# The exponential of the clipped source flow, made on VectorE from the tanh of both flows

## The reference

```python
conserved_sink   = sum((q + EPS) * (k_so_sum + EPS), -1) + EPS
conserved_source = clip(sum((k + EPS) * (q_si_sum + EPS), -1) + EPS, -1.0, 1.0)
sink_allocation    = sigmoid(conserved_sink)
source_competition = softmax(conserved_source, -1) * n      # over the tokens
v_comp = v * source_competition[..., None]
kv  = einsum('bhnd,bhnm->bhdm', k, v_comp)
out = einsum('bhnd,bhdm->bhnm', q_norm, kv) * sink_allocation[..., None]
```

## Time and profile before

| | |
|---|---|
| median of 3 runs | 2896.59 us (2896.01 to 2897.06) |
| the profiled execution, its own time | 2897.44 us |
| its span, from the first instruction to the last | 2895.7 us |
| outside of the span | 1.7 us |
| mean granted clock of TensorE | 0.944 |
| instructions | 67341 |

### The profile page before, as it was taken

How to read it: one execution, slowest core, us unless ns; L and a number is a source line. 1 busy time by engine, 2 the same in 40 slices (tenths; PEclk the granted TensorE clock), 3 DMA queues, 4 the chain that set the end, 5 groups by cost and what they waited for, 6 DMA issues and landing times. The chain is left out here.

```text
span 2895.7 us, 67341 instructions
## 1 busy us (share of the span) xinstructions
PE 2512.6 (87%) x26720; PEld 1816.3 (63%) x26720; DVE 2187.3 (76%) x3781; ACT 1440.4 (50%) x2616; POOL 704.7 (24%) x593
## 2 busy tenths in 40 slices
PE   4898889988898888998889979898798997989979
PEld 2666557665576656765667656676566765666646
DVE  4857778678777787776977769768697585985868
ACT  2755237552466434664256632567336572265813
POOL 1220332204322042220512205112152021520125
PEclk8999999999999999999999989999899998999989
DMA  5110211102111021110211112010120101201012
GB/s 218 38 37 2 84 48 38 37 2 95 37 38 37 2 99 34 41 34 6 98 30 45 30 38 73 26 46 27 41 76 27 45 19 52 66 29 48 14 55 70
DMA packets 93371, 136.26 MB, mean 47 GB/s; under 512 B 10111, under 2 KB 55240, under 8 KB 92552
## 3 DMA queue, kind: packets, MB, share of 16 engines
q1 hardware_dynamic: 84872, 115.16, 12.2%
q0 software_dynamic: 8192, 16.79, 1.9%
HBM read 101.31 MB, written 30.61 MB: 46 GB/s over the span
## 5 line engine op out<-in xcount | busy, mean ns | idle before, releaser
L1025 DVE TENSOR_REDUCE neg_max<-ps 128x1 f32<-128x1024 f32 x512 | 622.8, 1216 | 51.0 <-PE ps L1454 39.7
L700 ACT ACTIVATE probs<-ps,neg_max 128x1024 f32<-128x1024 f32 x512 | 571.1, 1116 | 158.2 <-DVE neg_max L1025 156.7
L1454 PE MATMUL ps<-keys,q_parts 64*128 64x512 f32 x3072 | 523.5, 448 | 82.7 <-ACT probs L700 56.6
L1331 PE MATMUL ps<-q_parts,w_split 128*128 128x512 f32 x1536 | 458.7, 434 | 68.7 <-DVE ffn L1147 41.0
L1331 PEld LDWEIGHTS ps<-q_parts,w_split 128*128 128x128 f32 x1536 | 281.7, 190 | 220.1 <-DVE ffn L1143 119.1
L599 POOL TENSOR_TENSOR probs<-ffn,q_parts 128x512 f32<-128x512 f32 x208 | 291.5, 1404 | 490.8 <-DMA q_parts<-gate_rows 276.9
L1475 PEld LDWEIGHTS ps<-ident,probs 64*128 64x128 f32 x8192 | 348.1, 143 | 96.0 <-ACT probs L700 17.2
L1454 PEld LDWEIGHTS ps<-keys,q_parts 64*128 64x128 f32 x3072 | 265.4, 196 | 220.8 <-ACT probs L700 108.3
L754 ACT ACTIVATE ffn<-ffn 128x512 f32<-128x512 f32 x256 | 159.9, 630 | 462.2 <-DVE ffn L1143 461.5
L1033 DVE COPY probsT<-ps 128x512 f32<-128x512 f32 x512 | 348.1, 680 | 23.6 <-PE ps L1475 23.6
L1475 PE MATMUL ps<-ident,probs 64*128 64x64 f32 x8192 | 350.2, 227 | 16.2 <-ACT probsT L682 16.2
(11 more groups left out here) (213 smaller groups left out, 3320.0 us busy)
## 6 DMA issues: line engine op xcount, KB each, us to landing
w_split<-w_parts SPq DMA_DIRECT2D x132, 256.0 KB, 2.6
q_parts<-gate_rows SPq DMA_DIRECT2D x64, 512.0 KB, 4.4
y_rows<-probs SPq DMA_DIRECT2D x40, 256.0 KB, 2.2
x_in<-in_x SPq DMA_DIRECT2D x9, 512.0 KB, 4.1
w_parts<-q_parts SPq DMA_DIRECT2D x2, 2048.0 KB, 14.4
out<-x_mid SPq DMA_DIRECT2D x8, 512.0 KB, 3.2
ffn<-in_gate_up SPq DMA_DIRECT2D x1, 2048.0 KB, 8.9
probsT<-in_gate_up SPq DMA_DIRECT2D x1, 2048.0 KB, 13.2
```

Of the source, the lines that this page charges most:

```text
L700: nc.scalar.activation(probs[:, t % 3, :], banks(2 * (t % 2)), ACT.Exp, bias=neg_max[:, t % 4:t % 4 + 1], accum_out=row_sum[:, g % 2, t % ...
L1025: nc.vector.tensor_reduce(neg_max[:, t % 4:t % 4 + 1], banks(2 * (t % 2)), X, ALU.max, negate=True).then_inc(max_ready.sem, 1)
L1331: mm = nc.tensor.matmul(ps[:, bank, :], w_split[:, f % CHUNK_SLOTS, h, k * P:(k + 1) * P], tokens[:, half], start=(part == 0), stop=(part ...
L1454: mm = nc.tensor.matmul(ps[:, 2 * (t % 2) + c, :], q_parts[rows, j, q, n * P:(n + 1) * P], keys[rows, k, :], start=(part == 0), stop=(part ...
```

## The change

ScalarE takes the tanh of both flows at once, in place, in one instruction of 256 columns, and no exponential. For the source flow, VectorE then works out `exp(x) = (1 + t) / (1 - t)` with `t = tanh(x / 2)`: `1 - t`, its reciprocal, and the product with `1 + t`. The clip to -1 and 1 keeps t away from 1. The sink's sigmoid stays as it was, now from the tanh in place, between the first and the second of the three. GpSimd's product of the values waits for the last of them, by a semaphore of its own.

```diff
-DVE_STEPS = 60
+DVE_STEPS = 61
...
-        flow_act = signal("flow_act", 2)
+        flow_act = signal("flow_act", 1)
+        source_ready = signal("source_ready", 1)
...
                     if u == FLOW_VALUES:
-                        pool.wait_ge(flow_act.sem, flow_act.at(b, 2))
+                        pool.wait_ge(source_ready.sem, source_ready.at(b, 1))
                         nc.gpsimd.tensor_tensor(heads(v_comp), heads(flow_v), per_head(source_exp), ALU.mult
...
                     if u == FLOW_ALLOC:
                         act.wait_ge(conserved_ready.sem, conserved_ready.at(b, 1))
-                        nc.scalar.activation(sink_alloc, conserved[:, 0, :], ACT.Tanh, scale=0.5
+                        nc.scalar.activation(conserved[:, :, :], conserved[:, :, :], ACT.Tanh, scale=0.5
                                              ).then_inc(flow_act.sem, 1)
-                        nc.scalar.activation(source_exp, conserved[:, 1, :], ACT.Exp).then_inc(flow_act.sem, 1)
...
                     if u == FLOW_VALUES:
                         dve.wait_ge(flow_act.sem, flow_act.at(b, 1))
-                        link(nc.vector.tensor_scalar(sink_alloc, sink_alloc, 0.5, 0.5, ALU.mult, ALU.add))
+                        nc.vector.tensor_scalar(source_exp, conserved[:, 1, :], -1.0, 1.0, ALU.mult, ALU.add)
+                        link(nc.vector.tensor_scalar(sink_alloc, conserved[:, 0, :], 0.5, 0.5, ALU.mult, ALU.add))
+                        link(nc.vector.reciprocal(source_exp, source_exp))
+                        nc.vector.scalar_tensor_tensor(source_exp, conserved[:, 1, :], 1.0, source_exp,
+                                                       ALU.add, ALU.mult).then_inc(source_ready.sem, 1)
```

## The result

| | before | after |
|---|---|---|
| median, beside each other on one chip | 2897.06 us (9 runs) | 2905.14 us (9 runs) |
| profiled execution, own time | 2897.44 | 2906.07 |
| its span | 2895.7 | 2904.3 |
| its mean granted clock of TensorE | 0.944 | 0.941 |

The changed kernel is slower: ratio 1.0025, interval 1.0013 to 1.0037. Two later comparisons, on the same kernels, gave 1.0022 (1.0010 to 1.0033) and 1.0014 (1.0006 to 1.0023). The forecast was "no difference", with 2896.2 and a range from 2892.0 to 2903.0.

A forecast was written before the change was run, and what follows sets the result against it. VectorE waits for ScalarE's silu at unit 15, but TensorE at unit 22 sets the batch. VectorE 0.43 us late against 0.48 slack: -0.05 a batch, -0.4 in eight, from 2896.59 to 2896.2 us; range 2892.0 to 2903.0.

The forecast's parts named there:

- slack before unit 22: TensorE, before unit 22's gate_up: could start at 371.18, waits until 371.66 for VectorE's L1147 of unit 20; 0.48 us.
- time at half clock: TensorE: twice (1 - mean clock) times the span, no forecast term; a line through all runs gives 0.31 us per us.
- The wait that goes: Unit 15: without ScalarE's two table loads the silu ends earlier, so VectorE's product starts 0.84 us earlier.
- The price of the operations: VectorE before unit 17: 1 - t 0.14, reciprocal 0.99, closing product 0.14; sum 1.27 us a batch.
- VectorE's lead behind GpSimd's product: Unit 16: GpSimd's L615 runs 0.54 us earlier, so VectorE's held product ends earlier and VectorE is 0.54 us ahead.
- The median as the kernel's time: Starting value of the sum: the median of three runs, 2896.59 us, with the runs' own spread of about 0.5.
- The rival in which GpSimd holds VectorE: Unit 15: GpSimd's L599 gets ahead and L1210 stands some 1.15 us; 8.8 us in all, 2905.4; chance 0.13.
- 0.78 for no difference: Whole kernel: chance of a time within 0.2% of before, 0.72 for the forecast plus 0.06 for VectorE's lead carrying.

The follow-up runs named there:

- the PSUM form: Changed kernel with 1 - t and its reciprocal in a PSUM bank: ratio 1.0084 to the kernel before; also without the reciprocal, 1.0032.
- the kernel without the exponential: The kernel before with tanh in the exponential's place, so both table loads go and VectorE gets no new operation: ratio 0.9986 to the kernel before.

## Why the prediction was wrong

The forecast failed in two places. The slack before unit 22 was mis-sized, which turned -0.4 us into +2.6; this alone would have left the time inside the range. The time at half clock was put at nothing, and it goes with the rest, which carried the total over 2903.0.

- **The wait that goes.** Right. ScalarE's tanh, the loads, the silu, and 0.84 us earlier on VectorE (0.83 measured).
- **The price of the operations.** Nearly: 1.27 forecast. L1210 to L1143 is 1.59 where it was 0.25 before, 1.34. The steps without and with a link are 0.14 and 0.25 as forecast, and the reciprocal has 0.95 as interpolated. The closing product stepped 0.21 and not 0.14. But the reading was too simple: without the reciprocal the same time goes by.
- **VectorE's lead behind GpSimd's product.** Right: L1143 of unit 18 is 7.92 after the tanh (365.58); by the forecast it was 7.88.
- **TensorE's slack before unit 22**, "0.48 us of slack": this is the step that failed. I set a gate_up free 0.46 after the down product's start, since that is where the next one's start is recorded. But the rows that I had show two kinds: 359.71 with 1.96 and the next product 1.80 behind, 362.74 with 1.63 and the next 1.47 behind (364.21). Comparing a start without a gap with one after a gap overstates the slack by the 0.33. It was 0.16: from unit 19's gate_up to unit 23's lie 12.96 us before and 12.80 after. With 0.16 the forecast's own sum is 0.43 - 0.16, 2.2 us in eight; with unit 19 really 0.50 late it is 0.50 - 0.16, and +0.33 was measured: 2.6 us, above the +1.8 of my bounds. On the starting value of 2896.59 that is 2899.2.
- **The median as the kernel's time.** The forecast started from three runs within 1.1 us. 89 further runs of the same kernel lie between 2892.2 and 2909.0, and their medians are 2899.7, 2899.3 and 2898.8. So the start was 2 to 3 us low. The range gave the runs 0.5 us (and its likeliest part is added up 0.2 off: -1.9 and +1.8 with 0.5 about 2896.59 reach from 2894.2 to 2898.9). The term that is missing is the time at half clock, which no part of the sum had: the changed kernel has 12 to 17 us more of it than the kernel before beside it, by the line above 4 to 5 us. Why it has more stays open.
- **The rival in which GpSimd holds VectorE** had the measured time almost to the microsecond (2905.4 against 2905.14), and for a wrong reason: L1211 was held in no batch. A total that fits is no evidence for the mechanism; the row of 0.22 us denies it. That it came so near is luck: with the slack of 0.16 its own sum is 1.58 - 0.16, 11.4 us in all, or 2908.0. But the price was right, as the PSUM form shows, and so was the 0.02 us by which it is avoided.
- **0.78 for no difference** was too sure. The stage alone would have been inside of 0.2%, at 0.09%.

## What to carry to other kernels

To read slack on TensorE, compare starts of the same kind, or the ends of the work: a product that follows another without a gap is recorded as started while the other still runs, here 0.33 us early. Before work is moved to VectorE, look at what GpSimd does at that time: here a tensor_scalar on an SBUF tile waited for the whole of a GpSimd product that had started 0.04 us earlier, and a product with two SBUF inputs for one that had started 0.23 earlier, while a reciprocal of 0.95 us beside it was free. And if the clock of TensorE moves between executions, a few microseconds gained or lost in one stage are not yet gained or lost in the total: print the time at half clock beside the total.

## What the runs showed that I had not expected

The reciprocal of 128 columns (0.95 us) costs nothing in the changed kernel: without it the time from unit 17 to 23 is 18.22 us instead of 18.23. Two starts on two engines, of which one moves by 0.06 us against the other so that their order turns, cost 1.18 us a batch. And the kernel without the exponential had single runs of 2877.1 and 2883.9 us beside nine at 2890.9 to 2899.9, at a mean clock of 0.953 and 0.949 against 0.941 to 0.945: the same program, up to 23 us apart, and the fastest runs have the highest clock.
